# The experts' outputs of a sparse mixture layer go back to the tokens by eight accumulating indirect DMAs, in place of one-hot matrix products

## The reference, cut to what matters

```python
gate_logits = _ffn(xf, gate_wi, gate_bi, gate_wo, gate_bo)
topv, topi = jax.lax.top_k(gate_logits, K)
topv = topv / jnp.sum(topv, axis=-1, keepdims=True)
onehot = (topi[..., None] == jnp.arange(E)).astype(x.dtype)
w = jnp.einsum('nk,nke->ne', topv, onehot)
h = jax.nn.selu(jnp.einsum('nh,ehf->enf', xf, exp_wi) + exp_bi[:, None, :])
out_e = jnp.einsum('enf,efh->enh', h, exp_wo) + exp_bo[:, None, :]
out = jnp.einsum('enh,ne->nh', out_e, w)
...
x = x + _L0_ffn_ref(_layernorm(x, axis=-1), ...)
```

## Time and profile before

| what | us |
|---|---|
| median of 3 runs | 216.96 |
| lowest, highest | 215.62, 220.72 |
| the profiled execution | 216.22 |
| its span, first to last instruction | 214.5 |

### The profile page before, as it was taken

How to read it: one execution, slowest core, us unless ns; L and a number is a source line. 1 busy time by engine, 2 the same in 40 slices (tenths; PEclk the granted TensorE clock), 3 DMA queues, 4 the chain that set the end, 5 groups by cost and what they waited for, 6 DMA issues and landing times.

```text
span 214.5 us, 6218 instructions
## 1 busy us (share of the span) xinstructions
PE 185.8 (87%) x2516; PEld 139.5 (65%) x2517; DVE 160.7 (75%) x409; ACT 112.9 (53%) x225; POOL 43.8 (20%) x59
## 2 busy tenths in 40 slices
PE   2788839887999999999999997999995799999961
PEld 2355518475977767777777754758770449988951
DVE  6489995899977796779687735666899755788484
ACT  3278863543344376436744689597701245876100
POOL 7353998000000204020302001420303200000000
PEclk9999996999699999999999999999999999999999
DMA  5983599218994878996000000000000000000006
GB/s 137 261 206 105 115 361 394 76 38 280 286 314 128 255 137 212 367 392 218 3 3 3 3 0 0 2 5 0 2 0 0 3 0 3 2 3 2 0 3 196
DMA packets 28005, 24.20 MB, mean 113 GB/s; under 512 B 8628, under 2 KB 22215, under 8 KB 27976
## 3 DMA queue, kind: packets, MB, share of 16 engines
q1 hardware_dynamic: 25944, 23.01, 35.9%
q10 hardware_dynamic: 2032, 0.79, 1.4%
HBM read 17.24 MB, written 1.31 MB: 86 GB/s over the span
## 4 chain that ended last, share of the span: by engine, by line
PE 44%; DVE 30%; ACT 11%; issue 6%; POOL 3%; DMA 2%; SPq 1%; DVEq 1%; ACTq 0%; POOLq 0%
PE pair L1122 8%; PE pair L1136 6%; PE pair L1161 5%; PE pair L1149 5%; PE pair L1358 4%; PE pair L1342 4%; DVE mx L810 3%; DVE PR L813 2%; ACT GR L628 2%; ACT GE L627 2%; PE pair L1324 2%; DVE i L850 2%; PE pair L1368 2%; DMA ebo_rows<-in_L_xattn_bv_dram 2%; ACT PR L598 2%
## 5 line engine op out<-in xcount | busy, mean ns | idle before, releaser
L1122 PE MATMUL pair<-BD,OH 128*128 128x64 bf16 x768 | 27.3, 199 | 3.1 <-DVE OH L728 2.7
L1122 PEld LDWEIGHTS pair<-BD,OH 128*128 128x128 bf16 x768 | 26.7, 102 | 4.8 <-DVE BD L802 3.5
L598 ACT ACTIVATE PR<-PR 128x1024 f32<-128x1024 f32 x16 | 16.9, 1056 | 24.1 <-DVE PR L813 24.1
L605 ACT ACTIVATE PT<-pair 128x512 f32<-128x512 f32 x32 | 17.5, 595 | 16.9 <-PE pair L1149 16.8
L810 DVE TENSOR_REDUCE mx<-pair 128x16 f32<-128x1024 f32 x16 | 19.3, 1208 | 3.1 <-PE pair L1136 3.0
L1136 PE MATMUL pair<-KD,QT 64*64 64x256 f32 x256 | 21.4, 409 | 0.1
L383 POOL TENSOR_TENSOR rstd<-vare,half_neg 128x4 f32<-128x4 f32 x8 | 9.0, 1131 | 60.9 <-DVE vare L762 51.5
L1161 PEld LDWEIGHTS pair<-VD,PT 128*64 128x64 f32 x512 | 16.3, 138 | 6.3 <-issue 6.3
L813 DVE TENSOR_TENSOR PR<-pair,mx 128x1024 f32<-128x1024 f32 x16 | 19.6, 1224 | 0.5
L1149 PE MATMUL pair<-ident,PR 128*128 128x128 f32 x128 | 17.4, 280 | 2.7 <-ACT PR L598 2.3
L1149 PEld LDWEIGHTS pair<-ident,PR 128*128 128x128 f32 x128 | 14.3, 142 | 5.8 <-ACT PR L598 5.0
(11 more groups left out here) (201 smaller groups left out, 352.0 us busy)
## 6 DMA issues: line engine op xcount, KB each, us to landing
BB<-bins_dram SPq DMA_DIRECT2D x16, 512.0 KB, 6.8
KD<-x2r SPq DMA_DIRECT2D x2, 2048.0 KB, 10.3
w_ei<-in_L_ffn_exp_wi_dram SPq DMA_DIRECT2D x8, 256.0 KB, 5.9
w_eo<-in_L_ffn_exp_wo_dram SPq DMA_DIRECT2D x8, 256.0 KB, 7.0
w_ei<-in_fside_BxSx_dram SPq DMA_DIRECT2D x8, 192.0 KB, 4.5
X<-in_x_dram SPq DMA_DIRECT2D x4, 256.0 KB, 6.4
KD<-KT SPq DMA_DIRECT2D x32, 32.0 KB, 2.5
out_dram<-X SPq DMA_DIRECT2D x4, 256.0 KB, 2.9
```

Source lines behind the costliest of these rows:

```text
L598: nc.scalar.activation(PR[:, t % 2], PR[:, t % 2], ACT.Exp).then_inc(exp_done, 1)
L605: nc.scalar.activation(PT[:, t % 2, 4 * half:4 * half + 4, :].rearrange("p c n -> p (c n)"), PTP[half][:, :], ACT.Copy).then_inc(pt_ev, 1)
L1122: mm(o, OH[:, t % 2, i * P:(i + 1) * P], BD[:, s], start=(i8_ == 0 and s == 0), stop=False, skip_group_check=True)
```

## The change

The output goes to HBM in two parts. SP stores `X` as soon as attention is done with it (`x2_done`), without the experts' part. The experts' part is added there by POOL: for each expert one indirect DMA takes the 128 rows of `Yw[:, e, :]` (512 bytes each) and adds them to the rows of `out` whose numbers stand in `row_i[:, e]`. Two experts can have the same token, and an accumulating DMA must not run beside another one on the same row; so POOL waits, after each one, until all 16 counts of `d_scat` have come, before it issues the next. It also waits once for `d_out`, that is for the plain stores.

The row numbers come along with the gather: two more label columns per expert in `XW` (partition, and 128 times the tile; `XWW` grows from 416 to 432), two more columns in the sums that give `wsl` (`SUMS` is 5 for 3). So that every one of the 128 slots of an expert has a row of its own, non-members are no longer moved out of reach but take the candidates' places and the slots behind the members (nine more small products in `places()`, two more ahead of it, one more DVE multiplication each); their weight is zero. Gone are all transposes of `G1` and `G2`, `GT1`, `GT2`, the split `Y3`, the scatter products, `OC` and its split, the back products and the additions to `X`. ACT takes no part in the weighing now: DVE does it in one instruction per expert, `weigh(e-2)` behind `selu(e)`.

Apart from that, `ones_row` and `ebo_rows` have 128 rows, zero beyond the second, so that the bias product reads through 128 rows; for this POOL clears `ebo_rows` when it is done with the gate's splits, SP loads the experts' biases after the stores, and ACT writes its row after `EBO_ZERO`.

```diff
             for g in range(NG):
-                sp.wait_ge(x_back[g], outer)
+                sp.wait_ge(x2_done, TG * (g + 1))
                 sp.dma_start(out_dram[:, tiles(g), :], X[:, tiles(g), :]).then_inc(d_out, 16)
+            sp.wait_ge(pool_const, EBO_ZERO)
+            sp.dma_start(ebo_rows[1:2, :, :], e_bo.rearrange("(a e) h -> a e h", a=1)).then_inc(d_eb, 16)
             sp.wait_ge(d_out, 16 * NG)
...
-            link(nc.gpsimd.memset(ones_row[:, :], 1.0 / SELU_SCALE))
+            link(nc.gpsimd.memset(ones_row[:, :], 0.0))
+            link(nc.gpsimd.memset(ones_row[0:2, :], 1.0 / SELU_SCALE))
...
+            nc.gpsimd.memset(ebo_rows[:, :, :].rearrange("p e h -> p (e h)"), 0.0).then_inc(pool_const, 1)
+            pool.wait_ge(pool_const, EBO_ZERO)
+            label = lambda s: XW[:, :, 3 * D + s * E:3 * D + (s + 1) * E]
+            link(nc.gpsimd.iota(Wt[:, :, :], [[0, T], [0, E]], base=0, channel_multiplier=1, allow_small_or_imprecise_dtypes=True))
+            link(nc.gpsimd.iota(Wr[:, :, :], [[P, T], [0, E]], base=0, channel_multiplier=0, allow_small_or_imprecise_dtypes=True))
+            nc.gpsimd.tensor_copy(label(3), Wt[:, :, :])
+            nc.gpsimd.tensor_copy(label(4), Wr[:, :, :])
+            nc.gpsimd.memset(minus_bf[:, :], -1.0)
+            nc.gpsimd.tensor_scalar(turn[:, :], lower[:, :], -2.0, 1.0, ALU.mult, ALU.add).then_inc(pool_const, 1)
+            pool.wait_ge(pool_const, LABELS)
             nc.gpsimd.memset(G1[:, :, :].rearrange("p t n -> p (t n)").bitcast(F32), 0.0).then_inc(g1_zero, 1)
...
+            pool.wait_ge(d_out, 16 * NG)
+            pool.wait_ge(cnt_done, 1)
+            outer = pool.value_load(cnt_i[0:1, 0:1], min_val=1, max_val=P // CAND)
+            inner = pool.value_load(cnt_i[0:1, 1:2], min_val=1, max_val=MAXRI)
+            with pool.Fori(0, outer) as ro:
+                with pool.Fori(ro * inner, ro * inner + inner) as k:
+                    pool.wait_ge(rows_done, k + 1)
+                    pool.sem_inc(pool_seen, 1)
+                    for e in range(E):
+                        pool.wait_ge(y_done, k * E + e + 1)
+                        pool.sem_inc(pool_seen, 1)
+                        pool.indirect_dma_start(out_rows, bass.IndirectOffsetOnAxis(row_i[:, e:e + 1], 0), Yw[:, e, :], None,
+                                                bounds_check=B * L - 1, compute_op=ALU.add).then_inc(d_scat, 16)
+
+                        pool.wait_ge(d_scat, k * (16 * E) + 16 * (e + 1))
+                        pool.sem_inc(pool_seen, 1)
...
-                        if e % 2 == 1 and e >= 3:
-                            weigh((e - 3) // 2)
-                    weigh(NY - 1)
...
+                    def weigh(e):
+
+                        dve.wait_ge(y_mm, k * E + e + 1)
+                        nc.vector.tensor_scalar(Yw[:, e, :], YB[e % 4][:, 0:D], wsl[:, e:e + 1], None, ALU.mult).then_inc(y_done, 1)
 
                     dve.wait_ge(ws_mm, k + 1)
-                    ilink(nc.vector.reduce_sum(wsl[:, :], OPS[:, 0:3 * E].rearrange("p (e s) -> p e s", s=3), AX.X))
+                    sums = OPS[:, 0:SUMS * E].rearrange("p (e s) -> p e s", s=SUMS)
+                    ilink(nc.vector.reduce_sum(wsl[:, :], sums[:, :, 0:3], AX.X))
                     nc.vector.tensor_scalar(wsl[:, :], wsl[:, :], SELU_SCALE, None, ALU.mult).then_inc(wsl_done, 1)
+
+                    ilink(nc.vector.reduce_sum(row_f[:, :], sums[:, :, 3:5], AX.X))
+                    nc.vector.tensor_copy(row_i[:, :], row_f[:, :]).then_inc(rows_done, 1)
                     dve.wait_ge(wsl_done, k + 1)
-                    evac_gt2(2)
                     selu(0)
-                    evac_gt2(3)
-                    for e in range(1, E):
+                    selu(1)
+                    for e in range(2, E):
                         selu(e)
-                        if e % 2 == 1 and e >= 3:
-                            weigh_rest((e - 3) // 2)
-                    weigh_rest(NY - 1)
...
+                    dve.wait_ge(d_scat, k * (16 * E) + 16 * E)
                     assert inn[0] == ISTEPS, inn
 
-                for q in range(NC):
-                    dve.wait_ge(back_mm, ro * NC + q + 1)
-                    nc.vector.tensor_tensor(X[:, tiles(q), :], X[:, tiles(q), :], BKB[q][:, :].rearrange("p (t h) -> p t h", t=TG), ALU.add).then_inc(x_back[q], 1)
-                for q in range(NC):
-                    dve.wait_ge(x_back[q], ro + 1)
-                dve.wait_ge(g1_tr, ro * 2 + 2)
+                dve.wait_ge(xc_mm, ro * NC + NC)
                 pick_candidates()
...
 
+                    past = PTP[0][:, 0:NC * E].rearrange("p (q e) -> p q e", e=E)
+                    mm(past, ident_bf[:, :], XW[:, 0:NC, 3 * D + 3 * E:3 * D + 4 * E], start=True, stop=False, skip_group_check=True)
+                    mm(past, ident_bf[:, :], XW[:, 0:NC, 3 * D + 4 * E:3 * D + 5 * E], start=False, stop=False, skip_group_check=True)
                     pe.wait_ge(mem_ev, ro + 1)
+                    for q in range(NC - 1):
+                        mm(past[:, q + 1:NC, :], minus_bf[:, :], memc[:, q:q + 1, :].broadcast_to([P, NC - 1 - q, E]), start=False, stop=False, skip_group_check=True)
+                    for q in range(1, NC):
+                        mm(past[:, 0:q, :], ones_bf[:, :], memc[:, q:q + 1, :].broadcast_to([P, q, E]), start=False, stop=False, skip_group_check=True)
+                    mm(past, turn[:, :], memc[:, :, :], start=False, stop=True, skip_group_check=True)
                     for q in range(NC - 1):
                         mm(MPS[:, (q + 1) * E:NC * E].rearrange("p (q e) -> p q e", e=E), ones_bf[:, :],
...
+                        if e >= 4:
+                            pe.wait_ge(y_done, k * E + e - 3)
+                        elif e >= 2:
+                            pe.wait_ge(rows_done, k + 1)
+                        o = YB[e % 4][:, 0:D]
...
-                    pe.wait_ge(gt1_ev, ro * 2 + 2)
-                    g2_transposes(0)
-                    g2_transposes(1)
+                        last.then_inc(y_mm, 1)
+
...
                     last.then_inc(ws_mm, 1)
-                    g2_transposes(2)
                     hidden(1)
-                    g2_transposes(3)
                     for e in range(2, E + 2):
                         if e < E:
                             hidden(e)
                         output(e - 2)
-                        if e == E - 1:
-                            scatter(0, 0)
-                            scatter(0, 1)
-                    for half in range(2):
-                        for i in range(1, NY - 1):
-                            scatter(i, half)
-                    for half in range(2):
-                        scatter(NY - 1, half).then_inc(sc_mm, 1)
-
...
+
+                    pe.wait_ge(y_done, k * E + E)
```

More of the change, by code:

```diff
@@ L95, in build @@
         ebi = sb("ebi", [P, E, FC], F32)
-        ebo_rows = sb("ebo_rows", [2, E, D], F32)
+        b_rows = sb("b_rows", [1, 5, D], F32)
         slot_iota = sb("slot_iota", [P, CAP], F32)
@@ L119, in build @@
         w_att = sb("w_att", [P, 4, D], F32, ab)
-        brow = ebo_rows[0:1, 0:5, :]
+        brow = b_rows[:, :, :]
         bcols = sb("bcols", [P, 4], F32, ab)
@@ L191, in build @@
         wsl = sb("wsl", [P, E], F32)
-        Yr = sb("Yr", [P, 2, 2, D], F32)
-        Y3 = sb("Y3", [P, 3, E, D], BF16)
+        ebo_rows = sb("ebo_rows", [P, E, D], F32)
+        turn = sb("turn", [P, P], BF16)
+        minus_bf = sb("minus_bf", [P, P], BF16)
+        row_f = sb("row_f", [P, E], F32)
+        row_i = sb("row_i", [P, E], I32)
+        Yw = sb("Yw", [P, E, D], F32)
         pair = [st.enter_context(nc.psum_tensor(f"pair{i}", [P, 1024], F32)) for i in range(4)]
@@ L243, in build @@
         d_x = [sem(f"d_x{g}") for g in range(NG)]
-        x_back = [sem(f"x_back{q}") for q in range(NC)]
         d_bb = [sem(f"d_bb{i}") for i in range(4)]
@@ L468, in _ @@
             link(nc.gpsimd.tensor_tensor(Wt[:, :, :], we[:, 0], we[:, 1], ALU.add))
-            w3 = [XW[:, :, 3 * D + s * E:3 * D + (s + 1) * E] for s in range(3)]
+            w3 = [label(s) for s in range(3)]
             link(nc.gpsimd.tensor_copy(w3[0], Wt[:, :, :]))
@@ L659, in _ @@
                         nc.scalar.activation(XG[:, i * 512:(i + 1) * 512], (OPS, MPS)[i][:, :], ACT.Copy).then_inc(xg_ev, 1)
-                    def weigh(i):
-                        if i == 0:
-                            act.wait_ge(wsl_done, k + 1)
-                        act.wait_ge(y_mm, k * NY + i + 1)
-                        for j in range(2):
-                            e = 2 * i + j
-                            last = nc.scalar.activation(Y3[:, 0, e, :], YB[i][:, j * D:(j + 1) * D], ACT.Identity, scale=wsl[:, e:e + 1])
-                        last.then_inc(y0_done, 1)
                     for e in range(E):
@@ L1301, in places @@
                        skip_group_check=True).then_inc(slot_mm, 1)
```

(20 more changed lines are left out.)

142 lines of the change are left out of this document (44 added, 98 removed).

## The result

The changed kernel takes 225.63 us in the median of four executions (224.9 to 227.75); the kernel before took 216.38 in four beside it. The ratio is 1.0456, with a 95% interval of 1.0371 to 1.0541: slower by 4.6%. Some executions of each kernel fall in a slower state; medians here are over all executions, ratios and intervals over the fast ones alone. The span of its profiled execution is 224.9 us, for 214.5 before.

What follows compares the result with a forecast made beforehand. It took a serial chain of eight waited-for POOL transfers as the bound: first weighing at 186.35, 8 x 4.0 us to 218.35, 1.4 us of leaving and picks, span 219.8, forecast 222 us, range 211 to 236.

Steps and rivals of the forecast that it cites:

- slower by over 2%: Whole kernel: outcome class of the forecast (0.50) and the one-off cost (0.06) together, chance 0.56.
- The serial chain as the bound: Tail behind the first weighing: eight POOL transfers, each waiting for the landing before, set the end: 8 x 4.0 us.
- d: Time from one `y_done` or landing to the next landing: 4.0 us, POOL's small instruction 1.1 plus a store 2.9.
- The lower bound of 2.4: Least d, from the fastest landing of a store of `X`, 2.4 us, if POOL's own part is free.
- The first weighing, 186.35: Expert loop: `y_done` for expert 0 comes at 186.35 us, as weigh(0) stands behind selu(2) on DVE.
- its own -0.2 us ahead of the experts: Stage ahead of the experts: clearing and transposes that go, against small products and a wider gather, sum near -0.2 us.
- The one-off cost at the first transfer: Rival at POOL's first transfer: first round late by as much as 6.1 us, time 228 us with d 4.0; chance 0.06.
- The bias rows: Expert loop on PE: bias product through 128 rows saves 0.14 us per expert, worth nothing as PE doesn't end the kernel.
- The stores of `X`: End of attention: they move to 128 us, behind the last addition at 127.79, hidden well ahead of the first scatter.
- The clearing of `ebo_rows` and the labels: POOL ahead of the experts: with `turn` and `minus_bf` some 3.3 us, hidden in a gap of over 10 us.

Runs made afterwards that it cites:

- own_targets: The changed kernel with eight scratch tensors as targets of the eight adding transfers and one wait at the end: one execution of 207.26 us, span 205.4.
- early_weigh: The changed kernel with weigh(e-2) ahead of selu(e) on DVE in place of behind it: ratio 1.0284.
- sp_plain: The changed kernel with plain 64 KB stores from SP to a scratch tensor, each behind the last landing, in place of POOL's indirect ones: round 1.73 us, span 205.3.
- copy_rows: The changed kernel with plain indirect writes in place of adding ones, waits, rows and bytes kept: round 3.27 us, landing 2.24.
- bias128_busy_pe: The kernel before with only the 128-row bias operands, plus 15 idle products in PE's two waits between gate and experts: ratio 0.9858, median 213.54 us.
- half_rows: The changed kernel with 64 rows per transfer in place of 128: mean round 4.03 us, for 4.36 with all rows.

## Why the prediction was right

It had 222 us, 211 to 236, and slower by over 2% as the likeliest case; measured were 225.6. The mechanism was right. That the number came so near is in part luck: inside the cost of one transfer two errors of 1 us and more stood against each other. The span was to be 219.8 and is 224.9, and the 5.1 us between them can be laid to its steps.

**The serial chain as the bound: right.** Every piece of the chain from 189.61 to 223.41 is a transfer or what stands between two, and behind that are 1.5 us of leaving the loop and picks, for the 1.4 foretold. `own_targets` shows that the waits, not the transfers, make it; `early_weigh` that what its start gains the end gains.

**d, sized 4.0, measured 4.36: near, but by other parts than were named.** From the first weighing, done at 188.56, to the last landing at 223.41 are 34.85 us, for 32 in the sum: 2.85 of the 5.1 us. I had 1.1 us for POOL and 2.9 for a store. A store of this size lands in 1.51 us (`sp_plain`), half of my 2.9: the median of stores of 256 KB was the wrong row, and so was the 2.2 of 32 KB from ACT. The sentence that the time "is plainly no matter of bytes" because these two differ by 0.7 us loses its ground with it: one store of 64 KB from SP took 1.51 us, where 256 KB took 2.9 (with four of them in flight). What filled the gap were a hand-over of 1.03 us between a landing and the next start, which my sum did not have, and the addition, 1.05 us, which I had taken to be mostly hidden. In the terms of the sum: POOL's part was 1.54 for 1.1, from its end to the landing were 1.8 us for 2.9, and 1.03 came on top. The errors nearly cancel, and this is the luck in the number. The lower bound of 2.4 was likewise no bound of a store; for the round as built it held.

The plain indirect write landed in 2.24 us (`copy_rows`), the adding one in 3.3, and the hand-over stands in neither. In the Trainium skill, "DMA: Bandwidth & Descriptors", section on the anatomy of one DMA on the gpsimd path, the fit gives, as an estimate, 2.15 us for 64 KB. The trace agrees with it for the plain write and not for the adding one; the section does not say of which of them it speaks. Eight rounds by the fit would have ended the span at about 205 us, as an estimate. With the waits in place no round of POOL's was that short: even the plain write has 3.27 us.

**The first weighing, 186.35, measured 188.56.** That is 2.2 us of the 5.1, and the order on DVE was read rightly: weigh(0) stands behind selu(2), and `early_weigh` gets 1.56 us back. The first transfer began 1.04 us behind the weighing, at 189.61, where the prediction had 186 to 187. From hidden(0) to the weighing are 7.85 us, and 7.88 in the prediction, whose sum left out its own -0.2 us ahead of the experts. So all of the 2.2 us lies ahead of hidden(0), which began at 180.72, at 178.47 before.

Two things came on top there. The gate ended 1.3 us later in this execution (the first counting product at 165.05, at 163.73 before). Most of it is one gap in attention, in which PE waited for nothing that the profile shows, and which the chain of before does not have:

```profile
102.47 1.18 issue
```

`bias128_busy_pe`, which stores `X` at the end, has 0.90 us at the same place, so the early stores are not what makes it; what does is open. In the eight profiles of the same program the first counting product begins anywhere from 162.28 to 165.46. The second thing is the fall of the clock, which no step of mine had. `own_targets` shows the way to hidden(0) without it:

```profile
164.22 0.22 PE L1260 MATMUL pair<-XW,ones_bf 128*128 128x128 bf16 x1 [2.31 <-DVE Ub L872]
...
178.21 1.16 PE L1320 MATMUL pair<-XG,w_ei 128*128 128x128 f32 x8 [0.96 <-ACT XG L680]
```

From the first counting product to hidden(0) are 13.99 us there (13.99 in `half_rows` too) and 15.67 in the profile of the changed kernel: 1.7 us for the clock. Before had 14.74, so the edits ahead of the experts gained 0.75 us and not 0.2. 1.3 and 1.7, less 0.75, are the 2.25 us.

**The one-off cost at the first transfer did not come.** The first transfer lands in 3.47 us and its part on POOL is 1.80 in place of 1.54; the distance to the second is 4.54. That is 0.2 us, not 6. The Trainium skill, "GPSIMD Engine Reference", section on instruction dispatch, has about 6 us for the first call of a freshly loaded routine. They do not show here; whether a routine was freshly loaded for this transfer no run shows.

**The bias rows: right that they are worth nothing here, wrong in size.** I put 0.14 us per expert by the bias product alone. It is 0.39, since the output product behind it also runs 0.20 us faster. The earlier trace rows had this: 1.09 us for the eight instructions of the output product and 0.89 for the eight of the hidden product, of one shape. Why the output product gains is open, but the rows showed that it might. The expert's period on PE came out at 2.01 us, not the 2.25 foretold, and the bias row of output(0) begins 4.28 us behind hidden(0) where before had 4.78. In the changed kernel these 3.1 us go into waiting; in the kernel before they are worth 1.6%.

**The stores of `X`** begin at 95.33 us and not near 128. Each group waits for its own four tiles only, and for its turn in SP's queue: the first two go at 95.33 and 96.53, when SP has issued the last loads of the experts (94.85), the third at 115.85, the last at 133.05, behind the last addition of attention at 132.73. The prediction took the addition at 127.79 in the trace of before for the last; it is the last but one, the last begins at 131.56. It cost nothing in the tail. The clearing of `ebo_rows` and the labels ended at 156.1, 9.3 us before POOL was wanted, as said.

## What to carry to other kernels

An accumulating transfer that must wait for the one before costs its whole landing and the hand-over each time, here 4.36 us against 1.84 to 2.11 for such transfers unwaited; so before moving work to an idle DMA queue, count the rounds that have to be serial, and look for a form in which the rows cannot collide (here candidates in place of experts). Price a waited-for transfer by a run of its own size and kind, and add the time between landing and next start. And split a change of two parts: the small one was worth 1.6% by itself, and was hidden by the large one.

## What the runs showed of the hardware

- Two PE rows of the same shape that differ in time, 0.89 and 1.09 us for eight instructions of 128x128 f32, pointed at the product in front of the slower one: with operands of 2 rows it cost 0.19 us itself and 0.20 in the next. Through 128 rows, mostly zeros, both are gone.
- An adding indirect transfer of 128 rows of 512 bytes: 1.54 us on POOL, 3.3 to the landing. A plain indirect one: 0.97 and 2.24. A plain store of the same bytes from SP: 1.51. 64 rows in place of 128 took 0.14 us off POOL's part. A round of waited-for ones is 4.36, 3.27 and 1.73 us.
- Between a landing and the next start POOL takes 1.03 us, SP 0.22; with nothing to wait for, 0.3 us lie between two of POOL's parts.
- The granted clock was 0.5 to 0.6 in the gather, behind two waits of PE, in six of eight profiles of one program up to that place, which cost 1.7 us or more, and 1.00 in the one profile with the waits filled.
